# A 16-head attention layer on Trainium2: ScalarE inverts the softmax totals as exp(-ln) in place of VectorE's reciprocal

## What is computed

```
x = x + causal 16-head attention(norm(x))          <- "causal"
x = x + 6-layer transformer stack(norm(x))         <- "stack"
x = x + single-head attention(norm(x))             <- "single"
x = x + the same stack again(norm(x))              <- "stack"
x = x + 16-head attention over the batch(norm(x))  <- "lead"
x = x + mixture of experts(norm(x))                <- "moe"
x = x + 16-head attention, binarised weights       <- "binary"
x = x + mixture of experts(norm(x))                <- "moe"
```

```
q, k, v = split_heads(norm(x) @ Wq, @ Wk, @ Wv)
scores  = q @ k.T * scale (+ mask in "causal")
attn    = softmax(scores)
y       = attn @ v, heads joined again
x       = x + y @ Wo
```

## Time and profile before

| | us |
|---|---|
| median of 3 runs | 4664.48 (4661.28 to 4667.9) |
| the profiled execution, its own time | 4656.89 |
| its span in the profile | 4655.1 |
| busy in the span: PE | 4075.6 (88%) |
| busy: POOL | 2999.5 (64%) |
| busy: DVE | 2885.5 (62%) |
| busy: ACT | 2678.4 (58%) |

### The profile page before, as it was taken

The page is one execution under the profiler, slowest core; times in us unless marked ns, Lnnn a source line. Parts: engine busy times, 40 slices in busy tenths (PEclk is TensorE's granted clock), DMA queues, the critical chain, the costliest instruction groups (busy, mean ns, idle before and its releaser), DMA issues.

```text
span 4655.1 us, 164467 instructions
## 1 busy us (share of the span) xinstructions
PE 4075.6 (88%) x67239; PEld 2843.3 (61%) x67239; DVE 2885.5 (62%) x4666; ACT 2678.4 (58%) x5529; POOL 2999.5 (64%) x1858
## 2 busy tenths in 40 slices
PE   7879999999999999977999999999999995457875
PEld 4546666666666666635666666666666662245644
DVE  5766666666666666734666766666666663516751
ACT  4546666666666666634666666666666663224542
POOL 0038888788888888815888888888887882420002
PEclk9989999999999999979999999999999997578987
DMA  2013333433334333311333343333333330040004
GB/s 67 1 38 92 101 98 87 107 94 99 97 88 105 92 100 97 89 45 46 95 100 96 92 106 93 97 101 92 106 88 98 100 88 12 0 121 3 1 9 121
DMA packets 349815, 367.90 MB, mean 79 GB/s; under 512 B 58737, under 2 KB 285042, under 8 KB 348786
## 3 DMA queue, kind: packets, MB, share of 16 engines
q1 hardware_dynamic: 338834, 348.92, 29.1%
q0 software_dynamic: 2048, 4.20, 0.3%
q10 hardware_dynamic: 8160, 3.93, 0.3%
HBM read 247.12 MB, written 109.71 MB: 77 GB/s over the span
## 4 chain that ended last, share of the span: by engine, by line
PE 58%; ACT 15%; issue 7%; DVE 5%; SPq 3%; POOL 3%; DMA 1%; ACTq 0%; DVEq 0%; POOLq 0%
PE banks L325 11%; PE banks L386 7%; PE banks L309 6%; PE banks L330 5%; PE banks L369 5%; PE banks L430 4%; PE banks L292 4%; PE banks L424 3%; ACT arena L461 3%; ACT ln_rs L467 2%; SPq L726 1%; ACT arena L480 1%; PE banks L880 1%; PE banks L340 1%; PE banks L352 1%
## 5 line engine op out<-in xcount | busy, mean ns | idle before, releaser
L637 POOL TENSOR_TENSOR arena<-arena 128x512 f32<-128x512 f32 x768 | 959.6, 1270 | 527.7 <-DVE arena L566 401.0
L642 POOL TENSOR_TENSOR arena<-arena 128x1024 f32<-128x1024 f32 x384 | 905.3, 2357 | 30.1
L639 POOL TENSOR_TENSOR arena<-arena 128x1024 f32<-128x1024 f32 x384 | 907.1, 2362 | 0.0
L325 PE MATMUL banks<-w_qk,arena 128*128 128x512 f32 x1536 | 736.3, 602 | 16.2 <-DVE arena L666 10.6
L440 ACT COPY arena<-banks 128x512 f32<-128x512 f32 x384 | 224.0, 583 | 808.2 <-PE banks L386 808.2
L566 DVE SCALAR_TENSOR_TENSOR arena<-arena,banks 128x512 f32<-128x512 f32 x768 | 493.6, 684 | 311.8 <-ACT arena L474 310.4
L559 DVE TENSOR_REDUCE arena<-arena 128x8 f32<-128x512 f32 x768 | 494.2, 679 | 84.0 <-ACT arena L456 83.9
L533 DVE TENSOR_REDUCE arena<-banks 128x8 f32<-128x512 f32 x384 | 265.0, 690 | 402.3 <-PE banks L309 398.6
L456 ACT ACTIVATE arena<-banks 128x512 f32<-128x512 f32 x768 | 447.2, 595 | 84.9 <-PE banks L325 72.6
L325 PEld LDWEIGHTS banks<-w_qk,arena 128*128 128x128 f32 x1536 | 277.8, 194 | 272.9 <-issue 272.9
L386 PE MATMUL banks<-ident,arena 128*128 128x128 f32 x3072 | 428.1, 283 | 16.7 <-POOL arena L642 15.5
(11 more groups left out here) (219 smaller groups left out, 6796.0 us busy)
## 6 DMA issues: line engine op xcount, KB each, us to landing
v_rows<-arena SPq DMA_DIRECT2D x1536, 64.0 KB
arena<-v_rows SPq DMA_DIRECT2D x768, 128.0 KB
arena<-v_rows SPq DMA_DIRECT2D x768, 112.0 KB
arena<-in_moe_w SPq DMA_DIRECT2D x30, 515.5 KB, 3.8
w_qk<-in_stack_qk SPq DMA_DIRECT2D x48, 256.0 KB, 3.0
w_v<-in_stack_v SPq DMA_DIRECT2D x48, 128.0 KB, 3.2
w_o<-in_stack_o SPq DMA_DIRECT2D x12, 512.0 KB
w_w<-in_stack_w SPq DMA_DIRECT2D x12, 341.0 KB, 3.3
```

The costliest lines, as they stand in the source:

```text
L325: pe.matmul(bank(M, tile), f.sh[:, (s // G) % 2, o:o + 128], w.qk[:, g], start=True, stop=True).then_inc(S.qk, 1)
L637: nc.gpsimd.tensor_tensor(f.sined[:, :, :, half, :], x[:, :, :, 1 - half, :], sines[:, :, mine].unsqueeze(1).to_broadcast([D, GH, 4, DH // ...
L639: nc.gpsimd.tensor_tensor(rot, x.rearrange("p h t a d -> p h t (a d)"), cosines.unsqueeze(1).to_broadcast([D, GH, 4, DH]), ALU.mult).then_ ...
L642: nc.gpsimd.tensor_tensor(rot, rot, f.sined.rearrange("p h t a d -> p h t (a d)"), ALU.add).then_inc(S.rotated, 1)
```

## The change

The layer's buffers get one more, `lg`. ACT's loop runs two steps longer. At every odd step from n = 5 on, ahead of its copy of pair n-2, ACT waits for `pv` of the block, takes the logarithm of the totals from bank 6 into `lg`, and exp(-lg) into `inv`. The wait for `divided` of the block before, which guards `inv`, goes to ACT with it. DVE drops the reciprocal and waits for ACT's `inverted` before its product.

```diff
-                         pt=(2, 4, 2 * T), ntop=(2, 4), inv=(T,), ot=(4, T), ...
+                         pt=(2, 4, 2 * T), ntop=(2, 4), lg=(T,), inv=(T,), ot=(4, T), ...
...
-    for n in range(PAIRS + 2):
-        if 0 <= n - 2:
+    for n in range(PAIRS + 4):
+        if 0 <= n - 5 and n % 2 == 1:
+            h = Pair(n - 5)
+            act.wait_ge(S.pv, h.block + 1)
+            nc.scalar.activation(f.lg, bank(M, 6)[:, T:2 * T], ACT.Ln).then_inc(S.logged, 1)
+            act.wait_ge(S.logged, h.block + 1)
+            if h.block >= 1:
+                act.wait_ge(S.divided, h.block)
+            nc.scalar.activation(f.inv, f.lg, ACT.Exp, scale=-1.0).then_inc(S.inverted, 1)
+        if 0 <= n - 2 < PAIRS:
             h = Pair(n - 2)
...
             h = Pair(n - 5)
-            dve.wait_ge(S.pv, h.block + 1)
+            dve.wait_ge(S.inverted, h.block + 1)
             if h.b >= 1:
                 dve.wait_ge(S.out_projected, h.b)
-            if h.block >= 1:
-                dve.wait_ge(S.divided, h.block)
-            nc.vector.reciprocal(f.inv, bank(M, 6)[:, T:2 * T]).then_inc(S.inverted, 1)
-            dve.wait_ge(S.inverted, h.block + 1)
             nc.vector.tensor_tensor(f.ot[:, h.c, :], bank(M, 6)[:, 0:T], f.inv, ALU.mult).then_inc(S.divided, 1)
```

More of the change, by code:

```diff
@@ L775, in heads_buffers @@
     return arena(M, dict(q=(T,), k=(2, T), qm=(2, 4, T), v=(2, 2, 16, 32), ones=(32,), p=(3, 2, 2, T),
-                         pt=(2, 4, 2 * T), ntop=(2, 4), inv=(T,), ot=(4, T), wraw=(4, D), sgn=(D,), neg=(D,), wsum=(4,),
+                         pt=(2, 4, 2 * T), ntop=(2, 4), lg=(T,), inv=(T,), ot=(4, T), wraw=(4, D), sgn=(D,), neg=(D,), wsum=(4,),
                          wpad=(4, D), wt=(3, D), wo=(4, D)))
@@ L1571 @@
 SINGLE_SIGNALS = """zeroed tok projected q k v q_masked scores maxed probs inverted normed turned pt pv residual"""
-HEADS_SIGNALS = """zeroed projected q k v q_masked scores maxed probs turned copied_first copied_second pv inverted
+HEADS_SIGNALS = """zeroed projected q k v q_masked scores maxed probs turned copied_first copied_second pv logged inverted
  divided out_projected residual"""
```

## The result

The changed kernel takes 4582.3 us (median of 4 runs, 4575.15 to 4593.69), the kernel before 4662.88 us beside it (4 runs, 4657.13 to 4667.9). The ratio is 0.9836, with a 95% interval of 0.982 to 0.9852: 80.6 us less, by the interval 69 to 84. The forecast was 4596, with a range of 4587 to 4622. In the profiled execution (4575.15 us) the span is 4573.3 us.

What follows compares the result with a forecast made beforehand. PE was taken to lead but wait for DVE's product, with the reciprocal in that loop. Waits 59.1, overlap 4.8, last value products 3.4 and last products 1.7 make 69.0 us; 4664.5 less 69 gives 4596, range 4587 to 4622.

Steps and rivals of the forecast that it cites:

- What bounds the kernel: Causal and binary modules: PE leads but waits 64.9 us ahead of its value products for DVE's product, not ACT's copy.
- The reciprocal's 1.75 is worth 1.18 in a plain causal block, since PE is next: Plain causal block: without the reciprocal, value product to value product falls from 6.90 to 5.72 us, PE's own work.
- the sum: Both modules: vanished waits 59.1, overlap 4.8, last value products 3.4, last products 1.7; together 69.0 us saved.
- The pair costs nothing: ACT, each block: logarithm and exponential, 0.9 us together, fit in the 1.37 us hole before the copy.
- The rival loop of 3.0 us plus the pair: ACT and PE, each block: value product, logarithm, exponential, copy, transposes; shorter than 5.72 until logarithm and exponential take 2.7 us.
- The ends of the modules: Last blocks of both modules: last value products start about 1.7 us earlier each, last products gain 0.8 to 0.9 each.
- still better: Module ends and layer norms behind: shorter last waits may keep the clock up, 1.3 us per last value product; chance 0.04.
- Other modules start when x is done and repeat their own rhythm, so they pass the gain on: Modules outside causal and binary: they pass on the gain, with no term of their own in the 69.0 us.
- The base of the forecast: Whole kernel before: the runs' median of 4664.5 us, 7.6 above the profiled execution, from which 69 was taken.
- the wait relabelled: Value products really wait for ACT's copy, so nothing is won: 4664 us; no change had chance 0.04.
- the pair on the path: Logarithm and exponential on ACT delay PE: 4640 to 4655 us with table loads, milder 4611 to 4640; partial gain 0.13.
- the slower clock: TensorE's granted clock falls in both modules as PE closes up; at a third lower 4710 us; slower had chance 0.04.

Runs made afterwards that it cites:

- the half reciprocal: Kernel before, causal and binary modules alone, with the reciprocal on only 128 of 256 columns: 543.5 us, against 588.53 with the whole reciprocal.
- both halves: Kernel before with logarithm and exponential on ACT replacing the reciprocal in the causal module alone, 4623.34 us, or the binary module alone, 4628.76 us.

## Why the prediction missed, step by step

- **What bounds the kernel: right.** The wait ahead of PV was for DVE's product, and the releaser "ACT copy" on the weight loads was not a cause; the half reciprocal showed it in proportion (0.80 off the reciprocal, 0.79 off the block).
- **The reciprocal's 1.75 is worth 1.18 in a plain causal block, since PE is next: right.** 5.72 forecast and measured; without any inversion 5.73. Over 31 blocks of each module the sum has 67.3 and the traces show 66.8.
- **The pair costs nothing: right.** 0.86 against the 0.9 estimated (0.40 and 0.42 with a hand-over of 0.04), in a hole that took up 1.94. The rival loop of 3.0 us plus the pair exists and starts to bind between 1.9 and 3.0.
- **The ends of the modules: right in kind, too small.** The waits shrank as said (2.87 to 1.07; 2.33 to 1.40). The sum left out that PE runs the work behind a shorter wait at the upper clock level: the last value product 2.79 to 1.51 in causal and 3.54 to 1.93 in binary, the last projection in binary 2.99 to 1.99. That is 3.9 us, as much as the two modules gave beyond 69.0 (72.1) and a little more. It stood in the forecast only as the case "still better", at 4%.
- **The step that failed: "Other modules start when x is done and repeat their own rhythm, so they pass the gain on", and with it the lower end of the range.** It puts what happens outside the two modules at nothing, and it left 9 us below the forecast for everything. The runs showed 5.0 us less there between the profiles: 2.8 less in the first stack and 3.4 in the single module, 2.0 more in the lead module. Together with the 3.1 at the ends, the 69 becomes 77 between the profiled executions; between the medians of all executions it is 79. In terms of the clock, a median moves by 4 us for each 0.001 of the mean granted clock, and the changed program's executions have 0.952 where those of before have 0.949. So the term that was mis-sized is the effect of the clock: nil in the sum, 10 to 12 us measured, a third of it at the ends of the two modules.
- **The base of the forecast** was a median of three, 4664.5; the median of all executions of the kernel before is 4661.8, which is 2.7 us of the miss.
- **The rivals:** the wait relabelled, the pair on the path and the slower clock did not happen. The clock did move, the other way than the rival "slower" had it.

What stays open is why the changed program has less time at the lower level outside the changed modules. Its modules begin earlier and end with shorter waits of PE, but the single module reads 68.7 and 68.8 in both halves, with the changed causal module ahead and with the old one, and no run here shows a cause.

## What to carry to other kernels

When an engine's instruction lies whole in a loop that the leading engine waits for, its worth is the wait, not its length: add up the leading engine's own spacings in a block without a wait, and the difference to the block with it is the gain. A chain added on another engine is free as long as its own loop, with all that is queued behind it, is shorter than that sum; lengthening it on purpose finds the slack. To see such a gain, measure from one instruction to the same one some blocks on: that repeated within 0.1 us in every profile here, while the medians of one program spread over 20 us. And where the median moves with the granted clock, look at executions at equal clocks too, but keep in mind that the change can move the clock itself, and make the range as wide as the clock's share on both sides.

## What the runs showed of the hardware

- A reciprocal on VectorE takes 1.75 us for 128x256 and 0.95 for 128x128; a logarithm on ScalarE 0.38 to 0.47, with a median of 0.40, for 128x256 from PSUM, and back to back eight of them take 2.31, 0.29 each. An exponential of it in SBUF takes 0.42.
- Two loads of the active table set a block cost 1.28 each with no drain to be seen beside them.
- Over 74 executions of the two full kernels the time moved by 4 us for each 0.001 of the mean granted clock. The kernel before alone spread over 23 us (4649.95 to 4672.87), over a quarter of the whole effect under test.
- The same module can hold a longer or a shorter stretch at the lower clock level from one execution to another: near the start of the binary module 41 us in the profiles of five runs and 20 to 24 in the other eleven, for 5 to 7 us of its time.
